# Residual image kept in DRAM between steps, and a dense channel-major buffer for the filter's output

## The reference

```python
residual = x
h = layer_norm(x, n1_g, n1_b)
xf = jnp.fft.rfft2(h, axes=(1, 2), norm='ortho')      # 128 x 65 frequencies
...                                                    # 8 blocks of 16 channels:
o1 = relu(complex_einsum(xf, w1) + b1)
o2 = softshrink(complex_einsum(o1, w2) + b2, 0.01)
h = jnp.fft.irfft2(o2, s=(H, W), axes=(1, 2), norm='ortho') + h
h = h + residual
residual = h
h = layer_norm(h, n2_g, n2_b)
h = jax.nn.gelu(h @ mw1 + mb1, approximate=False)      # 128 -> 512
h = h @ mw2 + mb2                                      # 512 -> 128
return h + residual
```

## Time and profile before

| what | value |
|---|---|
| median of three runs | 1863.12 us (1862.99 to 1868.97) |
| the profiled execution | 1863.78 us |
| its span, first to last instruction | 1862.0 us |
| PE busy | 1718.2 us, 92% |
| DVE busy | 1171.5 us, 63% |
| ACT busy | 946.6 us, 51% |
| POOL busy | 631.7 us, 34% |
| mean granted TensorE clock | 0.983 of 2.4 GHz |
| HBM | 36.92 MB read, 33.55 MB written |

### The profile page before, as it was taken

How to read it: one execution, slowest core, us unless ns; L and a number is a source line. 1 busy time by engine, 2 the same in 40 slices (tenths; PEclk the granted TensorE clock), 3 DMA queues, 4 the chain that set the end, 5 groups by cost and what they waited for, 6 DMA issues and landing times.

```text
span 1862.0 us, 34773 instructions
## 1 busy us (share of the span) xinstructions
PE 1718.2 (92%) x11184; PEld 1561.3 (84%) x11184; DVE 1171.5 (63%) x2879; ACT 946.6 (51%) x1778; POOL 631.7 (34%) x753
## 2 busy tenths in 40 slices
PE   0099998999999998999999999899999999899999
PEld 0099997888889997888889999688888999788888
DVE  7969726666657935666664971766664693556663
ACT  4335416666635623666653541566663562366665
POOL 4800003777740000677780000377775000011111
PEclk9999998999999998999999999999999999999999
DMA  7000001222210001222220000122221000011111
GB/s 196 6 1 1 1 15 44 68 68 68 69 46 1 1 1 36 62 69 68 68 68 13 1 1 6 47 70 72 68 68 46 1 1 0 8 32 36 34 34 46
DMA packets 128031, 71.71 MB, mean 39 GB/s; under 512 B 5090, under 2 KB 123236, under 8 KB 127940
## 3 DMA queue, kind: packets, MB, share of 16 engines
q1 hardware_dynamic: 127652, 70.03, 13.1%
q10 hardware_dynamic: 288, 0.46, 0.1%
HBM read 36.92 MB, written 33.55 MB: 38 GB/s over the span
## 4 chain that ended last, share of the span: by engine, by line
PE 87%; DVE 8%; POOL 2%; ACT 1%; issue 1%; DMA 1%; SPq 0%; DVEq 0%; POOLq 0%; ACTq 0%
PE ps L579 23%; PE ps L528 12%; PE ps L434 7%; PE ps L570 6%; PE ps L572 6%; PE ps L571 6%; PE ps L444 6%; PE ps L488 6%; PE ps L459 3%; PE ps L559 3%; PE ps L461 3%; PE ps L545 3%; PE ps L551 2%; DVE zbuf L837 1%; DVE pst L812 1%
## 5 line engine op out<-in xcount | busy, mean ns | idle before, releaser
L579 PEld LDWEIGHTS ps<-mw,gel 128*128 128x128 f32 x4096 | 533.2, 191 | 43.3
L579 PE MATMUL ps<-mw,gel 128*128 128x128 f32 x4096 | 536.4, 274 | 0.0
L1129 POOL TENSOR_TENSOR resid<-resid,mb2rep 128x512 f32<-128x512 f32 x128 | 163.0, 1273 | 1021.4 <-ACT hn L675 965.9
L689 ACT ACTIVATE gel<-ps,mb1f 128x512 f32<-128x512 f32 x512 | 351.8, 687 | 268.4 <-PE ps L572 237.3
L570 PE MATMUL ps<-hth,mw1h 128*128 128x512 f32 x512 | 262.7, 513 | 7.4 <-DVE htl L953 7.0
L675 ACT ACTIVATE hn<-resid,shift,rstd 128x128 f32 (+1 forms) x512 | 221.5, 483 | 38.7 <-DVE shift L1061 38.7
L528 PE MATMUL ps<-cst,spec 128*128 128x128 f32 x1024 | 225.2, 383 | 0.0
L528 PEld LDWEIGHTS ps<-cst,spec 128*128 128x128 f32 x1024 | 224.9, 313 | 0.1
L1122 POOL TENSOR_SCALAR zbuf<-xnext,rstd,shift 128x128 f32<-128x128 f32 x384 | 169.5, 461 | 157.6 <-DVE shift L1061 157.6
L434 PE MATMUL ps<-cst,zbuf 128*128 128x128 f32 x1024 | 129.8, 293 | 89.1 <-DVE zbuf L837 81.8
L936 DVE TENSOR_TENSOR resid<-ps,resid 128x512 f32 (+1 forms) x64 | 44.2, 691 | 264.4 <-PE ps L551 240.6
(11 more groups left out here) (93 smaller groups left out, 2506.8 us busy)
## 6 DMA issues: line engine op xcount, KB each, us to landing
between<-xout SPq DMA_DIRECT2D x62, 256.0 KB, 2.3
xnext<-between SPq DMA_DIRECT2D x62, 256.0 KB, 2.8
out_dram<-xout SPq DMA_DIRECT2D x62, 256.0 KB, 2.3
xnext<-in_x_dram SPq DMA_DIRECT2D x31, 256.0 KB, 2.8
mw1raw<-in_L_mw_dram SPq DMA_DIRECT2D x4, 256.0 KB, 2.5
mw<-in_L_mw_dram SPq DMA_DIRECT2D x4, 256.0 KB, 2.7
cst<-in_consts_dram ACTq DMA_DIRECT2D x1, 448.0 KB, 3.6
between<-xout SPq DMA_DIRECT2D x2, 192.0 KB, 2.1
```

The lines of the kernel that those rows point to most:

```text
L579: mm = pe.matmul(ps[:, r % 2, P * i:P * i + P], gel[:, r % 2, m, P * i:P * i + P], mw2[:, m, :], start=(m == 0 and i == 0), stop=(m == CHU ...
L689: act.activation(gel[:, r % 2, m, :], ps[:, 2 + m % 2], ACT.Gelu, bias=mb1f[:, m:m + 1]).then_inc(gelu_out, 1)
L1129: pool.tensor_tensor(t, t, b, ALU.add).then_inc(mb2_done, 1)
```

## The change

The three 64 KB arrays get other duties. Two of them, arena[0] and arena[1], change roles from step to step; the third, the work region, holds the input image at the start (first) and afterwards both the filter's temporaries and the MLP's buffers and weights.

| role in step s | before | after |
|---|---|---|
| normalised image z | zbuf | arena[s % 2] |
| spectrum (spec) | spec | arena[(s + 1) % 2] |
| filter output y | spec, laid out k, c, q | arena[s % 2], laid out q, c, k |
| output of idft_h (v) | zbuf | arena[(s + 1) % 2] |
| residual image | resid, stays | arena[s % 2], loaded from DRAM (aside) behind idft_h |

So y no longer shares the spectrum's memory, and the 128 frequencies of a channel lie side by side. A residual tile that POOL has made (in gz, four buffers instead of two) is stored to aside by SP (put_aside). In idft_h, as soon as a group of four channels is through PE, SP loads one residual tile over them; DVE waits for tiles 0 to 3, 4 to 7 and 8 to 31 ahead of pairs 0, 2 and 4. The input image of step 0 is stored aside in the same way, and ACT's first copy of the filter waits for the stores that cover its temporaries. POOL's add no longer waits for the output tile (x_out), and the last tile's add is POOL's as well. load_mlp waits for the filter's end instead of idft_h's. edges_out becomes two instructions. The core of the diff:

```diff
-        resid = sb("resid", [P, H, C])
-        zbuf = sb("zbuf", [P, H, C])
...
-        spec = sb("spec", [P, KWS, 2, 2, HALF])
-        yspec = spec[:, :, :, :, :].rearrange("p k a b d -> p (k a b d)").rearrange(
-            "p (k c q) -> p k c q", c=HALF, q=2)
...
+        first = sb("first", [P, H, C])
...
+            arena[i] = sb(f"arena{i}", [P, H, C])
+
+        flat = [a[:, :, :].rearrange("p h c -> p (h c)") for a in arena]
+        paired = [a.rearrange("p (t h e) -> p t h e", h=H, e=2) for a in flat]
+        spectra = [a.rearrange("p (k a b d) -> p k a b d", a=2, b=2, d=HALF) for a in flat]
+        columns_of = [a.rearrange("p (q c k) -> p q c k", q=2, c=HALF) for a in flat]
...
+        aside = nc.dram_tensor("aside", [IMAGES, TILES, W, ROWS, C], F32).ap()
...
+            for t in range(TILES):
+                if t < R_POOL0:
+                    sp.wait_ge(r_done, t + 1)
+                else:
+                    sp.wait_ge(r_dve, t - R_POOL0 + 1)
+                sp.dma_start(aside[0, slot_of(t)], first[:, ROWS * t:ROWS * t + ROWS, :]).then_inc(
+                    early_st if t < EARLY else late_st, 16)
+
+            def put_aside(s, j, r):
+
+                sp.wait_ge(r_done, R_POOL0 + TILES * s + 4 * j + r + 1)
+                to = aside[(s + 1) % 2, bass.ds(4 * j + r, 1)].rearrange("t w h c -> w (t h) c")
+                sp.dma_start(to, gz[:, r]).then_inc(gz_st[r], 16)
...
-                sp.wait_ge(ih_mm, CGROUPS * (s + 1))
+                sp.wait_ge(y_done, (UNITS + 1) * (s + 1))
                 load_mlp(layer)
...
+                for n in range(TILES):
+                    sp.wait_ge(ih_mm, CGROUPS * s + n + 1)
+                    sp.dma_start(resid_of(s)[:, ROWS * n:ROWS * n + ROWS, :], aside[s % 2, n]).then_inc(
+                        resid_in[min(n // 4, 2)], 16)
...
                             store(j - 1, r)
                             load(j, r)
+                            put_aside(s, j - 1, r)
...
-                                       yspec[:, :, ch, q], IH, start=True, stop=True)
+                                       y_of(s)[:, q, ch, :], IH, start=True, stop=True)
...
-                    act.wait_ge(r_done, R_POOL0 + TILES * s)
+                    act.wait_ge(x_out, X_CREDIT + TILES * s)
...
+                if s:
+                    for r in range(4):
+                        act.wait_ge(gz_st[r], 16 * (TILES // 4) * s)
+                else:
+                    act.wait_ge(r_done, R_POOL0)
+                    act.wait_ge(r_dve, R_DVE)
+                    act.wait_ge(early_st, 16 * EARLY)
...
-                    dst = yspec[:, bass.ds(2 * GROUP * b, 2 * GROUP), :, q]
+                    dst = y_of(s)[:, q, :, bass.ds(2 * GROUP * b, 2 * GROUP)]
+                dst = dst.rearrange("p c k -> p k c")
...
+                for r in range(2):
+                    ins = dve.tensor_scalar(dst[:, r], src[:, r], 0.5, None, ALU.mult)
+                ins.then_inc(y_done, 1)
...
-                if not last:
-                    dve.wait_ge(x_out, X_CREDIT + TILES * (s + 1))
-                    dve.wait_ge(gz_done, R_POOL0 + TILES * (s + 1))
-                    dve.tensor_tensor(resid[:, LAST:LAST + ROWS, :], xnext[:, 3], gz[:, 1], ALU.add).then_inc(
-                        r_done, 1)
...
+                dve.wait_ge(resid_in[0], RESID_IN[0] * (s + 1))
                 pair(0, 0)
...
+                dve.wait_ge(resid_in[1], RESID_IN[1] * (s + 1))
                 pair(1, 0)
                 pair(1, 1)
+                dve.wait_ge(resid_in[2], RESID_IN[2] * (s + 1))
...
-                        pool.wait_ge(r_done, R_POOL0 + TILES * s + m - 1)
-                        scale(h0, gz[:, r % 2])
-                    if again and known == TILES + 2:
-                        z_rows(j - 1, 3)
-                        pool.wait_ge(z_new, TILES * (s + 1))
-                        pool.wait_ge(r_done, R_POOL0 + TILES * s + m)
-                        scale(LAST, gz[:, 1])
-                    if again:
-                        pool.wait_ge(gz_done, R_POOL0 + TILES * s + m + 1)
-                        pool.wait_ge(x_out, X_CREDIT + TILES * s + m + 1)
+                        if s or m >= 4:
+                            pool.wait_ge(gz_st[r], 16 * (TILES // 4 * s + j - 1))
+                        scale(s + 1, h0, gz[:, r])
...
                     if again:
-                        residual(bass.ds(h0, ROWS), xnext[:, r], gz[:, r % 2])
-
-                for n in range(TILES + 3):
+                        pool.wait_ge(gz_done, R_POOL0 + TILES * s + m + 1)
+                        residual(gz[:, r], xnext[:, r], gz[:, r])
+
+                for n in range(TILES + 4):
```

More of the change, by code:

```diff
@@ L252, in afno @@
         row0_in, row0_st = sem("row0_in"), sem("row0_st")
+        early_st, late_st = sem("early_st"), sem("late_st")
+        gz_st = [sem(f"gz_st{i}") for i in range(4)]
+        resid_in = [sem(f"resid_in{i}") for i in range(3)]
         dve_own = sem("dve_own")
@@ L400, in _ @@
                         load(TILES // 4 - 1, r)
+                        put_aside(s, TILES // 4 - 2, r)
+                    for r in range(4):
+                        store(TILES // 4 - 1, r)
+                        put_aside(s, TILES // 4 - 1, r)
                 else:
@@ L404, in _ @@
                             store(j, r)
-                for r in range(4):
-                    store(TILES // 4 - 1, r)
+                    for r in range(4):
+                        store(TILES // 4 - 1, r)
             for i in range(2):
@@ L663, in v_out_ @@
                 act.wait_ge(ih_mm, CGROUPS * s + cg + 1)
[L664 removed]
+                evict_v(act.copy, s, cg, r).then_inc(v_act, 1)
             def normal(s, j, r, part):
@@ L709, in _ @@
                             a_out(s, q, j, r)
-                act.wait_ge(r_done, R_POOL0 + TILES * s)
-                act.wait_ge(r_dve, R_DVE)
+                if s:
+                    for r in range(4):
+                        act.wait_ge(gz_st[r], 16 * (TILES // 4) * s)
+                else:
+                    act.wait_ge(r_done, R_POOL0)
+                    act.wait_ge(r_dve, R_DVE)
+                    act.wait_ge(early_st, 16 * EARLY)
                 for q in range(2):
@@ L826, in _ @@
                     h = h0 + ROWS * t
-                    own.add(bn(resid, h, pst[:, h:h + ROWS, :]))
+                    own.add(bn(first, h, pst[:, h:h + ROWS, :]))
                 own.settle()
@@ L1082, in _, with scale, residual @@
                     build_spectral(STEPS[s + 1][0])
[L1083 removed]
+                last_tile(s)
         @block.gpsimd
         def _(pool):
[L1089 to L1095 removed]
+            def scale(s, h0, tmp):
+                pool.tensor_tensor(by_row(tmp), ztile(s, h0), gains(gain1[:, :]), ALU.mult).then_inc(gz_done, 1)
+            def residual(to, xtile, tmp):
+                pool.tensor_tensor(to, xtile, tmp, ALU.add).then_inc(r_done, 1)
             pool.wait_ge(gain_in, 16)
@@ L1105, in _ @@
                 h = slice(ROWS * t, ROWS * t + ROWS)
-                scale(ROWS * t, xout[:, t % 2])
+                scale(0, ROWS * t, xout[:, t % 2])
                 pool.wait_ge(gz_done, t + 1)
-                residual(h, resid[:, h, :], xout[:, t % 2])
+                residual(first[:, h, :], first[:, h, :], xout[:, t % 2])
             for s in range(len(STEPS)):
```

123 lines of the change are left out of this document (67 added, 56 removed).

## The result

The changed kernel takes **1782.57 us** (median of 4 runs, 1779.2 to 1787.48), the one before, run beside it, 1865.77 us: a ratio of 0.9556 with an interval of 0.9524 to 0.9587. It is faster by 4.4%. The time lies inside the predicted range, but 20.6 us above the predicted number, more than the runs scatter: a term of the sum was set wrongly.

What follows compares the result with a forecast made beforehand. PE, busy 92% of the span, was held bound at L528 by weight loads of columns 512 bytes apart. Sum: 1863.8 - 108.4 + 3 + 0.7 + 2.8 = 1761.9, forecast 1762 us, range 1752 to 1785.

Steps and rivals of the forecast that it cites:

- The dense loads: Inverse along h (L528): dense columns cut a step from 56.3 to 29.2 us, -108.4 us in four steps.
- the clock: Inverse along h: two steps begin at the 1.2 GHz level, no longer hidden by slow loads; +3 us, ends nothing and 8.
- The filter writes columns 512 bytes apart ... I take 0: Filter's last DVE operation (L891): writing single elements 512 bytes apart costs nothing; 0 us.
- The first rival: Filter's last DVE operation: the strided write costs, +36 to +56 us, total 1798 to 1818, middle 1808; chance 0.14.
- the nearest row: DVE's bn_stats (L812) reads 256 elements 512 bytes apart in 417 ns, against 427 ordinarily; taken as evidence for a free write.
- The rival's price: Filter's last DVE operation: PE's price, 0.85 ns an element, 434 ns an instruction, 0.28 to 0.43 us for 32 a step.
- a quarter of PE's price: Filter write: the range was extended beyond free writes to include this cost, up to 1785.
- the first case: Dense loads with free writes: total from 1753 to about 1773 us; chance 0.78.
- edges_out: DVE: two instructions of 128 elements instead of one of 256 cost 169 ns, four times, +0.7 us.
- The step ends: POOL's residual add ahead of tile 31's z rows delays PE 1.26 us at two ends, 0.3 at the middle; +2.8 us.
- Stores and loads at nothing: Residual tiles stored to DRAM and loaded back on the SP queue: both covered by other work, cost 0.

Runs made afterwards that it cites:

- e3: Against the change: y's layout keeps four channels side by side, writes in 16-byte runs, weight-load columns 16 bytes apart; 1886.72 us, one run.
- e5: Against the change: POOL's four z rows of tile 31 put ahead of the add of tile 30's residual again; 1780.64 us.
- e8: Against the change: filter result before and after the clamp kept channel-major, so the bias add reads PSUM at a distance and the last subtraction writes 32-byte runs; 1764.43 us.
- e1: Against the change: the last subtraction writes with k innermost, in 32-byte runs, and reads both inputs with 256 bytes between neighbours; 1827.78 us.
- e11: Against the change: only the clamped copy is channel-major, so clamp and last subtraction each have one input read 256 bytes apart; 1819.17 us, one run.
- e7: Against the change: the last subtraction's writes go to and fro between two neighbouring channels, its inputs read in pairs; 1796.32 us, one run.
- e4: Against the change: no stores of the residual image to DRAM, no loads back, no waits on them; 1786.79 us.
- e2: Against the change: y's layout keeps two channels side by side, writes in 8-byte runs, weight-load columns 8 bytes apart; 1773.7 us.

## Why the prediction was right, and where it was wrong

**The dense loads: right.** L590's loads have the median 192 ns that was named, the stage takes 28.7 us where 29.2 were taken, and the four steps give -109.1 us against -108.4 (-105.4 with the +3 for the clock). That a matmul at L528 was limited by its weight load is shown by e3 too: the same program with loads of 329 ns has a stage of 59.7 us.

**"The filter writes columns 512 bytes apart ... I take 0": wrong, and this is the step that failed.** The first rival's mechanism came true. L959 takes 366 ns more than L891. The filter of the change at full clock is 98.2 us long (step 3, and three steps of e5), the mean of the four before is 93.5; 4.7 us a step, 19 us in all, and e8, which takes the far write away and leaves the rest, gives back 18.1. The choice between the ends was made by "the nearest row", and the row was near in distance only: bn_stats shares the 512 bytes with L959, but neither the direction nor the two inputs nor the order (L959 comes back to a 16-byte piece only after 64 other elements), and e1 and e11 show that L959's own operation pays for far reads as well. The rule of the Trainium skill that the prediction quoted against this row (SBUF — State Buffer, Door 1, on cachelines) was right about the write.

**The rival's price was too high.** It put 434 ns on an instruction, from PE's loads, and 0.28 to 0.43 us on a round. Measured are 366 ns and some 0.19 us (2.65 to 2.84). Of the 366 ns, 0.14 us lies under the next operation, which begins before L959's record ends, so from its start to the next it is 0.91 instead of 0.69 us; and the steps between the round's other starts add up to 0.03 us less than before. And only some 24 of the 32 rounds of a step show it: in step 0 PE still keeps its rounds of 2.65 us up to 155, a third of the way into the filter. So the rival's +36 to +56 us became 19, and the time fell between forecast and rival.

That it fell inside the range is partly luck. The range had been stretched for a quarter of PE's price, 9 to 14 us, from an upper end of the first case that its own terms put at 1771.6 and not at 1773; the write cost more than that quarter, and the clock in the filter, below, was in no term. The profiled execution, 1787.48 us, lies above the range, the other three of the four inside it.

**The clock: its price for a stage about right, its place and its sum wrong.** Under L590 the prediction set +3 us for two steps that begin at 1.2 GHz. In the profiled execution one did, step 0's (first window below), and only for its first 1.8 us: it took 29.43 us instead of 28.69. In e7, where three stages begin at that level, each was 1.6 us longer, as reckoned (1.5). The larger loss came where the prediction named none: the clock fell in the filter of steps 1 and 2. Windows of the change at the start of step 0's inverse along h, then at the start of the filter in step 1:

```profile
223.43:225.20 1.77, 1.77 (x10) 1.77 (x10) 1.46 (x3) 0.00 (x0) 0.00 (x0) 0.50 0.00 0
...
546.00:549.00 3.00, 2.89 (x24) 2.69 (x24) 0.69 (x1) 1.45 (x5) 0.00 (x0) 1.00 0.00 0
549.00:552.00 3.00, 3.00 (x19) 2.34 (x17) 0.74 (x2) 1.39 (x3) 0.00 (x0) 1.00 0.02 5
552.00:555.00 3.00, 2.65 (x14) 2.31 (x13) 1.69 (x4) 1.28 (x3) 0.00 (x0) 0.64 0.00 0
555.00:558.00 3.00, 3.00 (x15) 3.00 (x15) 2.27 (x7) 0.61 (x2) 0.00 (x0) 0.50 0.00 0
...
564.00:567.00 3.00, 2.90 (x23) 2.44 (x22) 2.83 (x10) 1.47 (x3) 0.00 (x0) 1.00 0.00 0
```

At full clock PE was busy in 2.89 of 3 us, then with fewer matmuls, then in 2.65 as the filter's first rounds waited; there the clock went down to 0.50, the 1.2 GHz level, and came back by 564. Such a filter is 102.8 us long instead of 98.2. That makes the rest of the +29.4: 29.4 - 18.7 = 10.7 us, most of it in these two steps. Which stage it strikes differs between kernels: one filter of e4 (102.76 us), one of e8 (97.58), one of e5 (104.94), none of e2. Over all traces, 5 us or more at the lower level stand in 9 of the 24 filters of the six kernels whose last subtraction is slow, and in 4 of the 24 of the other six, none of them in the kernel before. So the slow subtraction may have a part in it; that was not tested, and why the clock falls where it does was not settled.

**edges_out** was forecast at 169 ns, and is 2 x 381 - 417 = 345 ns: the two halves write at the same distance and pay as well (in e2, where they write pairs, L980 takes 283 ns instead of 381). Four times that is 1.4 us instead of 0.7.

**The step ends: right in direction and in sum, not in the parts.** MLP and step ends together came out 3.1 us longer; +2.8 was forecast for the step ends. The parts were off: 0.75 us instead of 1.26 at the end of step 0, 0.77 at the end of step 2 (4.43 against 3.66), and 0.8 instead of 0.3 at the end of step 1 (PE idle 4.94 us before L482, 4.16 before the change):

```profile
939.75 1.01 PE L482 MATMUL ps<-vectors,w1s 64*128 64x1 f32 x4 [4.94 <-DVEq L864]
```

Over all traces the order of POOL's work is worth 1.23 us at the ends of steps 0 and 2 (e5 above), as forecast; the wait of step 1 varies by more than the term that was forecast for it, so that the sum came out so near is partly luck.

**Stores and loads at nothing: right.** e4 takes them away and is no faster; DVE has no wait on the loads.

With the write's 19 us put into the forecast, 1762 becomes 1781, within 2 us of the measured median. How near that comes says little: in the profiled execution the filter's clock adds 10.7 us and the inverse along h gives back 3.7, neither of them forecast, and the executions of the change spread over 8 us, with mean granted clocks from 0.977 in the slowest to 0.983 in the fastest.

One figure ahead of the prediction is a slip: three arrays of 64 KB are 128 x 384 floats a partition, not 128 x 512. No sum uses it.

## What to carry to other kernels

A transposition moves its price rather than removing it: look at the access order of each engine that touches the buffer in SBUF, and give every one of them at least two 4-byte elements in a row out of one 16-byte piece. Here the place where it was free was DVE's read of PSUM (e8), and a layout in pairs of channels (e2) served both the write and the load. When a cost is bounded by a nearby row, that row has to share the kind of operation, its operands and its direction, not only the stride; and of a longer instruction ask how much of it still shows from start to start.

## What was not expected of the hardware

- Columns 16 bytes apart load as slowly (median 330 ns for 128) as columns 512 bytes apart (313); columns 8 bytes apart take 196, dense ones 192.
- A subtraction of 512 elements on DVE costs 693 ns with both inputs in order and the result written 8 bytes apart (L891) or in runs of 8 or 16 bytes (e2, e3), and with runs of 32 bytes (e8), 1059 with single elements written 512 bytes apart, 1058 with one input read singly 256 bytes apart, 1296 with both inputs so. Going to and fro between two channels with the writes does not help (1070 in e7, with the reads in pairs).
- A read of PSUM with neighbours at least 256 bytes apart costs DVE nothing (684 ns, e8). The Trainium skill (SBUF — State Buffer, Door 1) has PSUM lines of 8 bytes and says that non-contiguous PSUM access slows matmuls; of DVE's read, L941 shows no slowdown.
